# Post-norm attention block with an int8 feed-forward layer: the late query chunks in another order, and what moves with them

## The reference, cut to what matters

```python
x = L0_attn_x                                  # (1, 4096, 256) float32, 16 heads of 16
ct_q  = x @ Wd_q_w + Wd_q_b                    # latent queries, 128 wide
query = ct_q @ Wu_q_w + Wu_q_b + rope(ct_q @ Wq_r_w + Wq_r_b, cos, sin)
ct_kv = x @ Wd_kv_w + Wd_kv_b                  # latent keys, 128 wide
key   = ct_kv @ Wu_k_w + Wu_k_b + rope(x @ Wk_r_w + Wk_r_b, cos, sin)
value = ct_kv @ Wu_v_w + Wu_v_b
attn  = softmax(query @ key.T / scale)         # per head, 4096 x 4096
x = layernorm(x + (attn @ value) @ Wo_w + Wo_b)
x = layernorm(x + int8_linear(x, weight_int8, weight_scale, bias))
```

## Time and profile before

| | |
|---|---|
| median of 3 runs | 1953.3 us (1953.26 to 1953.86) |
| the profiled execution | 1949.75 us |
| its span | 1947.9 us |
| ACT busy | 1802.0 us (93%) |
| PE busy | 1858.2 us (95%) |
| DVE busy | 1575.4 us (81%) |
| POOL busy | 162.5 us (8%) |
| mean granted TensorE clock | 0.984 |

### The profile page before, as it was taken

How to read it: one execution, slowest core, us unless ns; L and a number is a source line. 1 busy time by engine, 2 the same in 40 slices (tenths; PEclk the granted TensorE clock), 3 DMA queues, 4 the chain that set the end, 5 groups by cost and what they waited for, 6 DMA issues and landing times.

```text
span 1947.9 us, 31445 instructions
## 1 busy us (share of the span) xinstructions
PE 1858.2 (95%) x12996; PEld 452.8 (23%) x12996; DVE 1575.4 (81%) x1499; ACT 1802.0 (93%) x2022; POOL 162.5 (8%) x132
## 2 busy tenths in 40 slices
PE   8969999999999999999999999999999999999975
PEld 3331222122222222222222222222222112222234
DVE  4745988888888888888888888888988898888467
ACT  4349999999999999999999999999999999999945
POOL 5643700000000000000000000000000300000011
PEclk9989999999999999999999999999999999999987
DMA  4434111111011111111121011111121011111002
GB/s 140 151 110 167 26 25 25 26 26 25 20 19 21 18 26 26 26 25 25 25 64 30 14 18 20 25 25 26 26 47 25 17 20 18 22 26 25 1 24 87
DMA packets 161527, 73.67 MB, mean 38 GB/s; under 512 B 129984, under 2 KB 146624, under 8 KB 160896
## 3 DMA queue, kind: packets, MB, share of 16 engines
q1 hardware_dynamic: 158432, 67.12, 14.9%
q10 hardware_dynamic: 2944, 4.47, 0.8%
HBM read 49.39 MB, written 20.84 MB: 36 GB/s over the span
## 4 chain that ended last, share of the span: by engine, by line
ACT 61%; PE 22%; issue 10%; DVE 5%; DMA 1%; POOL 0%; SPq 0%; ACTq 0%; DVEq 0%; POOLq 0%
ACT arena L875 60%; PE PS L678 9%; PE PS L629 6%; PE PS L1152 4%; PE PS L718 1%; DVE arena L935 1%; PE PS L1301 1%; DMA arena<-tables_dram 1%; DVE bn L806 1%; DVE arena L931 0%; DMA arena<-xT_dram 0%; DVE arena L911 0%; DMA w<-weights_dram 0%; DVE absmax L1743 0%; DVE arena L1777 0%
## 5 line engine op out<-in xcount | busy, mean ns | idle before, releaser
L875 ACT ACTIVATE arena<-PS 128x1024 f32<-128x1024 f32 x1860 | 1708.1, 1336 | 16.2 <-PE PS L629 15.8
L678 PE MATMUL PS<-arena,Vh 128*32 128x512 f32 x8192 | 1092.9, 606 | 6.2 <-DVE arena L935 4.2
L629 PE MATMUL PS<-Qst,Kst 49*128 49x512 f16 x4096 | 728.6, 385 | 25.2 <-ACT arena L875 4.3
L935 DVE SCALAR_TENSOR_TENSOR arena<-arena 128x2048 f32<-128x2048 f32 x282 | 646.2, 2291 | 0.1
L911 DVE TENSOR_SCALAR arena<-PS 128x512 int32<-128x512 f32 x376 | 259.4, 690 | 252.4 <-PE PS L629 249.1
L629 PEld LDWEIGHTS PS<-Qst,Kst 49*128 49x128 f16 x4096 | 190.1, 93 | 1047.4 <-ACT arena L875 1020.6
L678 PEld LDWEIGHTS PS<-arena,Vh 128*32 128x32 f32 x8192 | 161.4, 108 | 314.9 <-issue 298.4
L931 DVE SCALAR_TENSOR_TENSOR arena<-arena 128x2048 f32<-128x2048 f32 x94 | 216.4, 2302 | 0.0
L919 DVE TENSOR_SCALAR arena<-arena 128x2048 int32<-128x2048 int32 x94 | 115.6, 1230 | 7.7 <-DVE arena L935 0.5
L921 DVE TENSOR_SCALAR arena<-arena 128x2048 int32<-128x2048 int32 x94 | 116.8, 1242 | 0.0
L1469 POOL TENSOR_SCALAR nmr<-mv 128x16 f32<-128x16 f32 x1 | 0.3, 263 | 1195.2 <-DVE mv L1633 1195.2
(11 more groups left out here) (118 smaller groups left out, 481.4 us busy)
## 6 DMA issues: line engine op xcount, KB each, us to landing
Kst<-k_halves SPq DMA_DIRECT2D x64, 128.0 KB
Qst<-q_halves SPq DMA_DIRECT2D x64, 128.0 KB
Vh<-head_values SPq DMA_DIRECT2D x30, 256.0 KB, 5.5
k_halves<-parts_or_sums SPq DMA_DIRECT2D x16, 256.0 KB, 2.6
q_halves<-parts_or_sums SPq DMA_DIRECT2D x16, 256.0 KB, 2.8
Kst<-k_halves SPq DMA_DIRECT2D x64, 64.0 KB
Qst<-q_halves SPq DMA_DIRECT2D x64, 64.0 KB
head_values<-arena SPq DMA_DIRECT2D x1, 4096.0 KB, 18.2
```

The source lines that it names most:

```text
L629: return nc.tensor.matmul(out, Kst[par][low:low + HK + 1, at:at + 128], Qst[par][low:low + HK + 1, j * CH:(j + 1) * CH], start=True, stop= ...
L678: last = nc.tensor.matmul(bank(value_bank(t))[32 * j:32 * j + 32, :], Vh[t % 2][:, kt, :], moving, start=kt == first, stop=kt == last_kt)
L875: nc.scalar.activation(ring(at, k), bank(g % SLOTS * SLOT, k), ACT.Exp, scale=EXP_SCALE).then_inc(a.exp, 1)
L935: last = nc.vector.scalar_tensor_tensor(out=t, in0=t, scalar=POLY[3 - j], in1=power if j == 3 else mantissa, op0=ALU.add, op1=ALU.mult)
```

## The change

- Late query parts come in the order 6, 7, 4, 5 on TensorE, ScalarE, GpSimd, VectorE and SP. Parts (6, q) and (7, q) use the tables which (6, k) and (7, k) used; only 4 and 5 are loaded again. The parts which use the buffers of the keys are now (4, q) and (5, q).
- SP issues the tables of chunk 4 ahead of the first stack (once (6, q) is turned), those of chunk 5 behind it, then stores the first shifts, then the query parts.
- DKV of a late chunk stands at the head of its own chunk and no longer between KR_ and DQ_ of the chunk before.
- The lengths of the second half of the keys come before QHI of chunk 7, which is now the sixth of twelve late query products. The transpose and the spreading matmul stand among the query products; VectorE does `key_row` and `key_column` right behind the key maxima, ahead of all late query parts. The first shifts are made after QHI of chunk 4, and `query_lengths(0)` comes after (6, q).

The diff, cut to what is used below:

```diff
+LATE = (HALF_CH + 2, HALF_CH + 3, HALF_CH, HALF_CH + 1)
...
-    late = range(HALF_CH, NCH)
-    order.append(("p", HALF_CH, DKV))
-    for c in late:
-        order += [("p", c, KR_)] + [("p", c + 1, DKV)] * (c + 1 < NCH) + [("p", c, DQ_), ("p", c, UK_), ("p", c, KHI)]
-    for c in late:
+    for c in range(HALF_CH, NCH):
+        order += [("p", c, e) for e in (DKV, KR_, DQ_, UK_, KHI)]
+    for c in LATE:
         order += [("p", c, QR_), ("p", c, UQ_), ("p", c, QHI)]
...
-TABLES = list(range(NCH)) + list(range(HALF_CH, NCH))
+TABLES = list(range(NCH)) + list(LATE[2:])
...
-        slot = ("k" if c >= NCH - 2 else n), c % 2
+        slot = ("k" if c in LATE[2:] else n), c % 2
...
             for c in range(HALF_CH, NCH):
-                next_tables(c, (c, "k"))
+                if c < NCH - 2:
+                    next_tables(c, (c, "k"))
                 store_parts(c, "k")
             for par in range(2):
                 sp.wait_ge(s_parts["k"][par], 32 * HALF_CH)
                 sp.wait_ge(s_parts["q"][par], 32 * (HALF_CH // 2))
+            next_tables(NCH - 2, (NCH - 2, "q"))
             load_stack(sp, fast.stack[0], 0, 0)
-            for c in range(HALF_CH, NCH):
-                next_tables(c + HALF_CH, (c, "q"))
+            next_tables(NCH - 1, (NCH - 1, "q"))
+            store_shift(0)
+            store_parts(LATE[0], "q")
+            sp.wait_ge(s_m, 16 * HALF_CH)
+            load_shift(sp, fast.stack[0], 0, 0)
+            for c in LATE[1:]:
                 store_parts(c, "q")
-                if c == HALF_CH:
-                    store_shift(0)
-                if c == HALF_CH + 1:
-                    sp.wait_ge(s_m, 16 * HALF_CH)
-                    load_shift(sp, fast.stack[0], 0, 0)
             load_stack(sp, fast.stack[1], 1, 1)
...
-                pe.wait_ge(s_dve, STEP["square", HALF_CH * half + HALF_CH - 1, n])
+                pe.wait_ge(s_dve, max(STEP["square", HALF_CH * half + c, n] for c in range(HALF_CH)))
...
-                if p == ("p", HALF_CH + 3, QHI):
+                if p == ("p", LATE[1], QHI):
...
-                if p == ("v", 0, 1):
+                if p == ("p", LATE[2], UQ_):
...
-                if p == ("v", 0, 4):
+                if p == ("p", LATE[3], QR_):
...
-                if p == ("v", 0, 5):
+                if p == ("p", LATE[2], QHI):
                     shifts(0)
...
                 if (name, n) == ("low", "k") and c == NCH - 1:
                     key_lengths(1)
-                if (name, n) == ("add", "q") and c == HALF_CH:
                     key_row()
-                if (name, n) == ("high", "q") and c == HALF_CH:
                     key_column()
-            query_lengths(0)
+                if (name, n) == ("low", "q") and c == LATE[0]:
+                    query_lengths(0)
```

More of the change, by code:

```diff
@@ L191 @@
 PARTS = [(c, n) for c in range(HALF_CH) for n in "kq"] + [(c, "k") for c in range(HALF_CH, NCH)] \
-    + [(c, "q") for c in range(HALF_CH, NCH)]
+    + [(c, "q") for c in LATE]
 ROTATED = {p: 3 * (n + 1) for n, p in enumerate(PARTS)}
-TABLES = list(range(NCH)) + list(range(HALF_CH, NCH))
+TABLES = list(range(NCH)) + list(LATE[2:])
 def tables_of(c, n):
-    return c if n == "k" or c < HALF_CH else c + HALF_CH
+    return c if n == "k" or c not in LATE[2:] else c + HALF_CH
 def make_slots():
@@ L221, in make_vector_steps @@
         steps += [("square", c, n) for n in "kq"] + [("low", c, n) for n in "kq"]
-    for n in "kq":
-        steps += [(name, c, n) for c in range(HALF_CH, NCH) for name in ("add", "high", "square", "low")]
+    for c, n in PARTS[2 * HALF_CH:]:
+        steps += [(name, c, n) for name in ("add", "high", "square", "low")]
     return steps
```

## The result

| | before | after |
|---|---|---|
| median of the runs | 1953.58 us (1953.26 to 1954.15, 4 runs) | **1934.05 us** (1932.91 to 1935.27, 4 runs) |
| the profiled execution | 1949.75 us | 1935.27 us |
| first exponential starts | 142.16 us | 126.07 us |
| last exponential starts | 1865.25 us | 1848.80 us |

The ratio is 0.9902, with a 95% interval of [0.9889, 0.9915]: the change gains 19.5 us by the medians. The two profiled executions lie 14.5 us apart, and why that is less than 19.5 is one of the things to settle. Of the 17 executions of the kernel before that ran beside b_again, a_again, a_wait13 and a_own_tables, one took 4390.6 us and counts as slow; it is left out of their ratios.

What follows compares the result with a forecast made beforehand. ScalarE's 1860 exponentials pace the middle, so only their start could move. The terms brought the first 16.8 us earlier; a new wait at the thirteenth left a gain of 14.2: 1953.3 - 14.2 = 1939.1 us, range 1935.5 to 1943.8.

Steps and rivals of the forecast that it cites:

- Term 5: Start of the exponentials: first at 125.4, thirteenth held until 140.8 by a new ScalarE wait of 2.5 us; gain 14.2 us.
- Rival 1: Landing of the stored shifts doesn't bind the thirteenth exponential, which runs at 138.3; gain 16.8 us, time 1936.5; chance 0.12.
- Term 1: Latent keys (DKV) one place later: TensorE's waits for x go, all 6.4 us; VectorE done with (7, k) at 94.9.
- The step from the profile to the median: Profiled execution forecast at 1935.5; before's lay 3.6 us under its median, a difference taken to carry over: 1939.1 us.
- Term 2: SP's queue: chunk 4's tables go first, stack starts at 99.4 instead of 104.9, chunk 5's tables land at 115.4.
- Term 3: One part, (5, q), behind the tables: 4.0 us on VectorE, last low at 123.4 instead of 134.8.
- Term 4: Earlier key maxima, row and column on VectorE and TensorE cost nothing; TensorE doesn't wait for the squares of (7, k).

Runs made afterwards that it cites:

- b_again: The kernel before, unchanged, run again: 1951.82 us, ratio 0.9988 to before.
- a_again: The kernel after, unchanged, run again: 1934.25 us, ratio 0.9894 to before.
- a_wait13: The kernel after with ScalarE's wait for the stored shifts and second stack really put before the thirteenth exponential: 1935.94 us, ratio 0.9906 to before.
- a_own_tables: The kernel after with tables of their own for chunks 4 and 5, loaded early into the second stack's buffers: 1932.75 us, ratio 0.9891 to before.
- b_warm_tail: The kernel before with 60 dummy matmuls added behind the last output projection in the final stage: 1953.92 us, ratio 1.0002 to before.
- a_max_back: The kernel after with key lengths, transpose, row, column, first shifts and check back at their places of before: 1940.2 us, ratio 0.9934 to before.
- a_check_back: The kernel after with only the check, query_lengths(0), put back behind the last query part: 1939.59 us, ratio 0.9931 to before.

## Why the prediction missed, by its own steps

**Term 5, start of the exponentials: this step failed.** The first exponential came at 126.07 (125.4 forecast), and the path to it, tables, GpSimd, one part and ScalarE, held. But "the thirteenth waits for the second stack and the second half of the shifts" is false; these waits are never issued. I gave it 2.5 us on ScalarE and took 14.2 for the gain where the thirteenth shows 16.4 (155.04 to 138.65). Rival 1 has the right thirteenth (138.3) and the gain of 16.8, with the wrong reason: it had the landing come earlier, and the landing came at 140.7, 0.1 us from the forecast. What separates the two is the experiment with the wait made real.

**Term 1, latent keys: right in kind, mis-sized.** No wait for x is left, as forecast. I took 6.4 us from one execution; by the medians DKV's place is worth 8.1 to 8.4. The load of x for chunk 6, 4.2 us in the earlier trace rows, takes 3.9 to 4.4 in the four profiles, but the one for chunk 7 takes 3.6 to 5.5. So the second wait is 2.1 to 4.0 us, and with it the second slow stretch comes or stays away. The cover is also thinner than the 8.6 us of my sum, which counts from the last product of the chunk before. The load is issued only at that product's evacuation, and ScalarE stood 5.0 us for a low of VectorE ahead of it:

```profile
73.84 0.45 ACTq L968 DMA_DIRECT2D arena<-xT_dram  x1
```

This x landed 4.6 us later, at 78.45, and its first product started at 80.36: 6.5 us of cover, 1.9 of them unused. At the other end of the term, (7, k) was done at 96.3 and not at 94.9. GpSimd began it at 87.31 (87.6 forecast) but was through at 92.8, 5.5 us where it had 3.9 before, because VectorE now worked on (6, k) beside it:

```profile
87.31 1.60 POOL L1449 TENSOR_TENSOR arena<-arena 32x512 f32<-32x512 f32 x1 [1.11 <-DMA arena<-arena]
88.88 1.71 POOL L1450 TENSOR_TENSOR arena<-arena 32x512 f32<-32x512 f32 x1
90.67 2.13 POOL L1452 TENSOR_TENSOR arena<-arena 32x512 f32<-32x512 f32 x1
```

The same operations take 1.25 us each without VectorE beside them. These 1.4 us are not the 1.2 by which the stack started late: the store of (7, k) landed at 99.2, but the table of chunk 4, which now stands ahead of the stack in SP's queue, waited until (6, q) was turned at 99.9. GpSimd needed 4.8 us for that part, from 95.2, where I had 3.9.

**The step from the profile to the median failed too, and it is the larger part of the miss.** I wrote that the profiled execution of before "lay 3.6 us under the median, and the difference is what carries over". It makes up 4.8 of the 5.1 us between 1939.1 and 1934.05. The difference does not carry over: it came from slow stretches behind x waits that the change removes, so the kernel after has no such difference at its start. Here the profiled execution is 1.2 us above the median. The profiled execution itself was forecast at 1935.5 and took 1935.27, and that is luck: the wait that isn't there (2.2 us at the thirteenth) and the final stage, which I had the same and which came 2.0 us longer, cancel. Profile to profile the gain is 16.4 us at the exponentials less 2.0 in the final stage, 14.4 by the spans; median to median it is 19.5. Of the 5 us between the two, 1.7 to 3.3 are seen at the first exponential of other executions of before. b_warm_tail, 3.5 us above the first profile of before, has all of these 3.5 us by its last exponential. The final stage of the profiled executions makes up 2.0 more. That the final stage of unprofiled runs is shorter isn't shown by a trace. What is on record is the mean granted clock of every run: of the nine runs of after and a_again it is 0.986 in the three that took 1935.3 us or more, and 0.987 to 0.988 in the six shorter ones. So this part of the account stays open; the ranges of the kernel before, 1950 to 1955 in twelve runs of b_again and 1951 to 1959 in those beside them, show how wide it is.

**Term 2, SP's queue: right.** The stack began at 100.6 (99.4) and the tables landed at 115.9 (115.4), 15.2 us after the stack's first issue against 16.0 taken from before. GpSimd waited 5.9 us for them rather than some 11: it was still turning (4, q) until 110.1. That wait still set the end.

**Term 3, one part behind the tables: right.** (5, q) took from 119.86 to 123.94, 4.1 us where I had 4.0; the low ended 0.5 us behind the forecast 123.4. By the rule of the Trainium skill (SBUF — State Buffer, "SBUF: two separate sides"), as I applied it, the three copies would have added their full time. They ran from 119.7 to 121.5, beside it, and took 0.57, 0.61 and 0.60 us:

```profile
112.40 0.68 DVE L1543 TENSOR_TENSOR arena<-arena 128x512 f32<-128x512 f32 x1
...
119.86 0.97 DVE L1543 TENSOR_TENSOR arena<-arena 128x512 f32<-128x512 f32 x1 [4.11 <-POOL arena L1452]
120.93 1.15 DVE L1548 CAST parts_or_sums<-arena 128x1024 f16<-128x1024 f32 x1
```

(4, q), from 112.40 with GpSimd idle, took 3.3 us (its steps are 0.68, 0.69, 0.69 and 1.22), so the copies added 0.7 us, all of it in the two steps beside them (0.97 and 1.15 us against 0.68 and 0.69), and not their 1.8. VectorE and GpSimd do hold each other up, but the trace disagrees with the sum that I had made of the rule. Beside turning a part takes 6.5 to 7.2 us, which is twice its time alone.

**Term 4, the maxima: right at nothing** for row, column and shifts (a_max_back against a_check_back). That TensorE would not wait for the squares of (7, k) was wrong: it waited 1.12 us at 95.26, since that part came late. a_max_back, which asks for them later, gains nothing by it. The check's earlier place is worth 3.8 to 4.4 us at the first exponential and 5.3 by the medians. I named that TensorE's wait at the entry would go but gave it no price of its own: it is hidden in term 5, "only ScalarE's shifts and the Exp table are left".

Put together, by the first exponential: 142.2 to 145.5 in before (b_warm_tail among them), 135.1 with DKV moved, 130.3 to 130.5 with the order of the chunks and of SP's loads in addition, 126.1 to 126.7 with the early check: 7 to 10, 5 and 4 us.

## What to carry to other kernels

Evaluate a guard with the program's own numbers before a forecast rests on it; a wait that stands in the source may never be issued, and the listing of each engine's instructions with the semaphores it waits for says so at once. When one execution lies beside the median, look for what in it varies from run to run (here a clock fall behind a short wait), and ask whether the change removes that, before carrying the difference over. A wait that ends last hides the next pace behind it: the tables' wait of 5.9 us was worth 1.9 when it went, because VectorE and GpSimd working side by side were right behind.

## What was not expected of the hardware

- One load of x, for chunk 7, took 3.60, 5.03, 5.14 and 5.49 us in the four profiles of kernels that wait for it. The wait of 2.06 us behind the shortest was followed by no fall of the granted clock. The seven waits of 2.37 to 3.95 us in these profiles were, each time at a cost of 1.6 to 1.7 us on eight matmuls. In the final stage two waits close together, 2.9 to 3.0 us and then 2.2 to 2.5, after 60 dummy matmuls did it too, as one of 15.6 had done.
- After nearly the same idle time, 15.7 us in before and 15.6 in after, the clock came back 1.0 us behind the start of the 24 products in one profile and 4.2 in the other, worth 1.5 us. The repeated executions gave nearly the same again (3.23 against 3.26 us for the group, 4.77 against 4.80).
- The load of 32 x 2 x 512 tables behind the eight stack loads takes 10.4 us in after and 11.3 in before, and 10.1 to 11.3 in all eleven profiles that have it there; its landing follows the stack's first issue by 14.9 to 16.0 us. The same load ahead of the stack took 3.0 us in after.
